# Two-layer transformer step on one Trainium2 core: the routed experts' rows gathered and combined in the experts' stage instead of a stage of their own

## What is computed

```python
xn = _layernorm(x, axis=-1)
s = _L1_attn_ref(xn)               # attention across the batch
g = _silu(_L1_ffn_ref(xn, ...))    # eight experts, two for each row
x = x + s * g
...
top_vals, top_idx = jax.lax.top_k(probs, K)            # K = 2 of E = 8
top_vals = top_vals / jnp.sum(top_vals, axis=-1, keepdims=True)
act = jax.nn.silu(h1) * h3
expert_out = jnp.einsum('tef,ehf->teh', act, w2)
y = jnp.einsum('te,teh->th', w_full, expert_out)       # weighted sum of the two
```

## Time and profile before

| | before |
|---|---|
| median of three runs | 1500.3 us |
| the profiled execution's own time | 1499.98 us |
| its span, first to last instruction | 1498.2 us |
| PE busy | 1346.3 us, 90% |
| DVE, ACT, POOL busy | 702.3, 565.6, 612.0 us |
| mean granted TensorE clock | 0.950 of full speed |
| last matmul ends, last gather is issued | 1441.34 us, 1485.96 us |

### The profile page before, as it was taken

The page is one execution under the profiler, slowest core; times in us unless marked ns, Lnnn a source line. Parts: engine busy times, 40 slices in busy tenths (PEclk is TensorE's granted clock), DMA queues, the critical chain, the costliest instruction groups (busy, mean ns, idle before and its releaser), DMA issues. The chain is left out here.

```text
span 1498.2 us, 25022 instructions
## 1 busy us (share of the span) xinstructions
PE 1346.3 (90%) x7870; PEld 1147.5 (77%) x7871; DVE 702.3 (47%) x1622; ACT 565.6 (38%) x1775; POOL 612.0 (41%) x518
## 2 busy tenths in 40 slices
PE   6989899999999999999885679999999999999940
PEld 6934487878787878887654569999999999999930
DVE  6452376666676766667636432223223222232236
ACT  3421276655556656655543321111212211112124
POOL 0010155444444545455426345172662617441135
PEclk9999899999999999999987789999999999999975
DMA  8025710000000000000015465373773828555247
GB/s 290 1 84 163 280 71 15 15 14 14 14 14 14 14 23 19 14 14 16 8 60 207 163 228 184 106 241 115 231 245 95 271 69 290 178 161 182 72 130 253
DMA packets 67069, 171.47 MB, mean 114 GB/s; under 512 B 6448, under 2 KB 15040, under 8 KB 66704
## 3 DMA queue, kind: packets, MB, share of 16 engines
q0 software_dynamic: 25776, 98.73, 19.8%
q1 hardware_dynamic: 35632, 61.95, 12.8%
q10 hardware_dynamic: 5616, 10.23, 1.9%
HBM read 125.26 MB, written 45.61 MB: 114 GB/s over the span
## 5 line engine op out<-in xcount | busy, mean ns | idle before, releaser
L1721 PE MATMUL bank<-expert_weights,rows_t 128*128 x1872 | 358.9, 347 | 2.1 <-DVE rows_t L1653 1.6
L1721 PEld LDWEIGHTS bank<-expert_weights,rows_t 128*128 128x128 f32 x1872 | 340.2, 189 | 6.1 <-issue 2.9
L989 ACT ACTIVATE room<-bank,room 128x256 f32<-128x256 f32 (+1 forms) x512 | 208.8, 415 | 115.5 <-DVE room L902 115.4
L1017 POOL TENSOR_TENSOR room<-room 128x1024 f32<-128x1024 f32 (+1 forms) x128 | 187.9, 1468 | 119.1 <-DVE room L879 119.1
L753 PE MATMUL bank<-room 96*128 (+2 forms) x1024 | 189.1, 327 | 0.0
L1665 DVE TENSOR_TENSOR x_keep<-x_keep,bank 128x400 f32<-128x400 f32 x78 | 44.5, 571 | 303.9 <-ACT x_keep L1608 302.6
L1131 POOL TENSOR_TENSOR expert_weights<-x_keep,expert_weights 128x1600 fp32r<-128x1600 f32 (+2 forms) x49 | 160.2, 3270 | 54.2 <-DMA expert_weights<-w 53.9
L753 PEld LDWEIGHTS bank<-room 96*128 96x128 f32 x1024 | 159.0, 191 | 13.7
L1744 PE MATMUL bank<-expert_weights,act_t 128*128 x702 | 165.6, 389 | 1.0 <-ACT act_t L1613 1.0
L1028 POOL TENSOR_TENSOR room<-room 128x256 f32<-128x256 f32 x128 | 93.1, 728 | 172.3 <-DVE room L963 171.1
L1744 PEld LDWEIGHTS bank<-expert_weights,act_t 128*128 128x128 f32 x702 | 131.5, 188 | 25.6 <-issue 1.3
(11 more groups left out here) (235 smaller groups left out, 1770.9 us busy)
## 6 DMA issues: line engine op xcount, KB each, us to landing
x_keep<-w POOLq DMA_DIRECT2D x28, 800.0 KB, 5.1
expert_weights<-w POOLq DMA_DIRECT2D x28, 800.0 KB, 6.5
x_keep<-w POOLq DMA_DIRECT2D x14, 768.0 KB, 5.7
expert_weights<-w POOLq DMA_DIRECT2D x14, 768.0 KB, 7.4
rows_by_expert<-room SPq DMA_DIRECT2D x1, 9984.0 KB, 29.1
x_keep<-rows_by_expert SPq DMA_DIRECT2D x39, 256.0 KB, 3.9
results_by_row<-x_keep ACTq DMA_DIRECT2D x39, 256.0 KB, 4.5
room<-wo SPq DMA_DIRECT2D x16, 512.0 KB, 5.7
```

What stands on the lines that cost most here:

```text
L989: last = sc.activation(Pr[:, m % 4, hh, 0:w], scores_bank(m)[:, w * hh:w * hh + w], ACT.Exp, bias=nb[:, par, hh:hh + 1], accum_out=sm[:, p ...
L1017: g.tensor_tensor(pr, pr, rs[:, one[1] % 2].unsqueeze(2).broadcast_to([P, 4, w]), ALU.mult).then_inc(normed, 1)
L1721: last = mm(psum(2 * hf + w)[:, 0:HF], xgT[:, par, of_x, P * k:P * k + P], W[:, ds(off + (of_w * SLOT + (k * 2 + w) * FF + hf * HF), HF)], ...
```

## The change

Stage `combine` goes. Its work stands in the experts' block, behind or beside the last blocks:

- A row's two places are stored in order of size, the lower expert's first (`s.slots`, two operations where there was one); its two weights are put in the same order by eight small DVE operations at the end of `across_batch`.
- Five more small DVE operations there make `s.landed`: how many results of even and of odd blocks have landed in DRAM when all before the last expert's have, and when all blocks in use have.
- POOL, behind its last weight chunk: when the results of all experts but the last have landed, it gathers the lower expert's rows of the 16 tiles into `z`, two gathers and then a wait for them; then it loads the attention results; when all blocks in use have landed, it gathers the first six tiles' rows of the higher expert, waits for the last block's `y_done`, and gathers the other ten.
- x1 is loaded by SP instead of POOL: one tile when the last rows are turned, three when the last activations are, the other twelve into buffers that come free as the tiles are added, each issued between two stores of the output.
- ACT scales six tiles ahead of the last block's copy out of PSUM and the other ten among the silus. DVE's three operations for a tile are those of before. `z`, the attention results and seven of the gathers' buffers lie over the first weight place.
- SP fills `ys` with zeros behind `xs`, and POOL's scatter waits for both. ACT's waits on `y_in` start from 16 more.

```diff
+                  ("by_parity", NBLK + 1),
...
+    put("by_parity", np.tile(np.concatenate([np.arange(0, NBLK + 1, 2), np.arange(1, NBLK + 1, 2)]), (P, 1)))
...
+        s.landed = s.carve(2, 2, dt=I32)
...
-        s.kept = sb(ctx, "kept", [P, 2, NT, D])
+
+        s.first_place = sb(ctx, "late", [P, 2 * SLOT])
         experts(s)
-        s.room(sb(ctx, "room3", [P, 10000]))
-        combine(s)
...
             sp.dma_start(s.xs.rearrange("(n p) h -> p n h", p=P),
                          zeros.unsqueeze(1).broadcast_to([P, NBLK, D])).then_inc(s.blank, 16)
+            sp.dma_start(s.ys.rearrange("(n p) h -> p n h", p=P),
+                         zeros.unsqueeze(1).broadcast_to([P, NBLK, D])).then_inc(s.blank, 16)
...
-            pool.wait_ge(s.blank, 16)
-            pool.wait_ge(slots_ready, 1)
+            pool.wait_ge(s.blank, 32)
+            pool.wait_ge(slots_ready, 2)
...
-            step(v.tensor_reduce(slotf[:, :, 0], small1, AX.X, ALU.add))
-            step.then(v.tensor_reduce(slotf[:, :, 1], small2, AX.X, ALU.add))
-            v.tensor_copy(s.slots, slotf).then_inc(slots_ready, 1)
+            step(v.tensor_reduce(slotf[:, 0], small1, AX.X, ALU.add))
+            step.then(v.tensor_reduce(slotf[:, 1], small2, AX.X, ALU.add))
+            v.tensor_tensor(s.slots[:, :, 0], slotf[:, 0], slotf[:, 1], ALU.min).then_inc(slots_ready, 1)
+            v.tensor_tensor(s.slots[:, :, 1], slotf[:, 0], slotf[:, 1], ALU.max).then_inc(slots_ready, 1)
...
+            ranked = s.gatew.rearrange("p t k -> p k t")
+            step(v.tensor_tensor(swap[:, 0], slotf[:, 0], slotf[:, 1], ALU.is_gt))
+            step(v.tensor_tensor(swap[:, 1], slotf[:, 0], slotf[:, 1], ALU.is_gt))
+            step(v.tensor_tensor(keep[:, 0], slotf[:, 0], slotf[:, 1], ALU.is_lt))
+            step.then(v.tensor_tensor(keep[:, 1], slotf[:, 0], slotf[:, 1], ALU.is_lt))
+            step(v.tensor_tensor(crossed[:, 0], ranked[:, 1], swap[:, 0], ALU.mult))
+            step(v.tensor_tensor(crossed[:, 1], ranked[:, 0], swap[:, 1], ALU.mult))
+            step.then(v.tensor_tensor(keep, ranked, keep, ALU.mult))
+            step(v.tensor_tensor(ranked, keep, crossed, ALU.add))
+
+
+            step(v.tensor_copy(until[:, 0:1], starts[:, E - 1:E]))
+            step.then(v.tensor_tensor(until[:, 1:2], starts[:, E - 1:E], n_blocks[:, E - 1:E], ALU.add))
+            step.then(v.tensor_tensor(below, until.unsqueeze(2).broadcast_to([P, 2, NBLK + 1]),
+                                      const("by_parity").unsqueeze(1).broadcast_to([P, 2, NBLK + 1]), ALU.is_gt))
+            step.then(v.tensor_reduce(n_below, below.rearrange("p i (r n) -> p i r n", r=2), AX.X, ALU.add))
+            step(v.tensor_scalar(s.landed, n_below, 16.0, 16.0, ALU.mult, ALU.add))
...
+    place = s.first_place
+    S = place[:, 0:NT * D].rearrange("p (t n) -> p t n", n=D)
+    z = place[:, NT * D:2 * NT * D].rearrange("p (t n) -> p t n", n=D)
+    def in_tiles(r):
+        return [r[:, i * D:i * D + D] for i in range(r.shape[-1] // D)]
+    higher = (in_tiles(place[:, 2 * NT * D:]) + in_tiles(stage.rearrange("p i n -> p (i n)")) +
+              in_tiles(s.carve(2 * D)) + [xg[:, 0]])
+    assert len(higher) == NT
+    x1_at = [xg[:, 1]] + in_tiles(act_.rearrange("p i n -> p (i n)"))
+    X1 = len(x1_at)
+    x1_at += higher[:NT - X1]
+    lower_in, scaled, gated, done, stored = (sem(n) for n in ("lower_in", "lower_scaled", "c_gated", "c_done", "stored"))
+    summed = sem("higher_added")
+    higher_in = [sem(f"higher_in{t}") for t in range(NT)]
+    x1_in = [sem(f"x1_in{i}") for i in range(X1)]
+    SCALED_FIRST, BESIDE_LAST = 6, 6
...
-            end = pool.value_load(s.ends[0:1, E - 2:E - 1], min_val=1, max_val=NBLK + 1)
-            pool.wait_ge(y_done, end)
-            pool.nop(nofuse=True)
+            def blocks_landed(which):
+                for par in range(2):
+                    n = pool.value_load(s.landed[0:1, which, par:par + 1], min_val=16, max_val=16 * (NBLK // 2 + 2))
+                    pool.wait_ge(y_in[par], n)
+                    pool.nop(nofuse=True)
+            def bring_rows(to, t, k, landed):
+                nc.gpsimd.indirect_dma_start(
+                    out=to, out_offset=None, in_=s.ys,
+                    in_offset=bass.IndirectOffsetOnAxis(ap=s.slots[:, t, k:k + 1], axis=0)).then_inc(landed, 16)
+            blocks_landed(0)
+            for t in range(NT):
+                bring_rows(z[:, t], t, 0, lower_in)
+                if t % 2 == 1:
+                    pool.wait_ge(lower_in, 16 * (t + 1))
             for q in range(NT // 2):
-
-                pool.wait_ge(y_done, NBLK - NT // 2 + q)
-                for i, rows in enumerate((s.x1, s.messages)):
-                    pool.dma_start(s.kept[:, i, 2 * q:2 * q + 2],
-                                   rows[2 * P * q:2 * P * q + 2 * P, :].rearrange("(t p) n -> p t n", p=P)).then_inc(
-                                       s.kept_in, 16)
+                pool.dma_start(S[:, 2 * q:2 * q + 2],
+                               s.messages[2 * P * q:2 * P * q + 2 * P, :].rearrange("(t p) n -> p t n", p=P)).then_inc(
+                                   s.kept_in, 16)
+            pool.wait_ge(s.converted, 1 + (E - 1) * NCH)
+            blocks_landed(1)
+            for t in range(NT):
+                if t == BESIDE_LAST:
+                    pool.wait_ge(y_done, NBLK + 1)
+                bring_rows(higher[t], t, 1, higher_in[t])
...
+            sp.sem_inc(y_in0, 16)
+            sp.sem_inc(y_in1, 16)
...
-            sp.wait_ge(y_in0, 16 * (NBLK // 2 + 1))
-            sp.wait_ge(y_in1, 16 * (NBLK // 2))
+            def bring_x1(t):
+                sp.dma_start(x1_at[t], s.x1[P * t:P * t + P, :]).then_inc(x1_in[t % X1], 16)
+
+            sp.wait_ge(x_turned, NBLK)
+            bring_x1(0)
+            sp.wait_ge(a_turned, NBLK)
+            for t in range(1, X1):
+                bring_x1(t)
+            for t in range(NT):
+                if t + X1 < NT:
+                    sp.wait_ge(summed, t + 1)
+                    sp.wait_ge(x1_in[t % X1], 16 * (t // X1 + 1))
+                    bring_x1(t + X1)
+                sp.wait_ge(done, 2 * t + 2)
+                sp.dma_start(s.out[P * t:P * t + P, :], z[:, t]).then_inc(stored, 16)
+            sp.wait_ge(y_in0, 16 + 16 * (NBLK // 2 + 1))
+            sp.wait_ge(y_in1, 16 + 16 * (NBLK // 2))
+            sp.wait_ge(stored, 16 * NT)
...
-                    act.wait_ge(y_in[1 - par], b * 8 - 8 if par == 1 else b * 8 - 16)
+                    act.wait_ge(y_in[1 - par], b * 8 + 8 if par == 1 else b * 8)
...
+            def scale(t):
+                sc.activation(z[:, t], z[:, t], ACT.Copy, scale=s.gatew[:, t, 0:1]).then_inc(scaled, 1)
+            act.wait_ge(lower_in, 16 * NT)
+            for t in range(SCALED_FIRST):
+                scale(t)
             result(NBLK, 1, False)
+            for t in range(NT):
+                if t + SCALED_FIRST < NT:
+                    scale(t + SCALED_FIRST)
+                act.wait_ge(summed, t + 1)
+                sc.activation(z[:, t], z[:, t], ACT.Silu).then_inc(gated, 1)
...
+            dve.wait_ge(s.kept_in, 16 * (NT // 2))
+            def add_higher(t):
+                dve.wait_ge(scaled, t + 1)
+                dve.wait_ge(higher_in[t], 16)
+                v.scalar_tensor_tensor(out=z[:, t], in0=higher[t], scalar=s.gatew[:, t, 1:2], in1=z[:, t],
+                                       op0=ALU.mult, op1=ALU.add).then_inc(summed, 1)
+            add_higher(0)
+            for t in range(NT):
+                if t + 1 < NT:
+                    add_higher(t + 1)
+                dve.wait_ge(gated, t + 1)
+                v.tensor_tensor(z[:, t], z[:, t], S[:, t], ALU.mult).then_inc(done, 1)
+                dve.wait_ge(done, 2 * t + 1)
+                dve.wait_ge(x1_in[t % X1], 16 * (t // X1 + 1))
+                v.tensor_tensor(z[:, t], z[:, t], x1_at[t], ALU.add).then_inc(done, 1)
...
-def combine(s):
...
```

More of the change, by code:

```diff
@@ L129, in build @@
         s.maskb = sb(ctx, "maskb", [P, P], BF16)
-        tables = sb(ctx, "tables", [P, 6 * NT + 2 * NBLK + E])
+        tables = sb(ctx, "tables", [P, 6 * NT + 2 * NBLK + E + 4])
         s.X = sb(ctx, "x_keep", [P, NT, D])
@@ L1149, in across_batch @@
     starts, of_block, odd = s.carve(E), s.carve(NBLK), s.carve(NBLK)
+    slotf, swap, keep, crossed = (s.carve(2, NT) for _ in range(4))
+    until, below, n_below = s.carve(2), s.carve(2, NBLK + 1), s.carve(2, 2)
     n_blocks = s.carve(E)
@@ L1163, in across_batch @@
     before_e, row_starts = s.carve(E, E), s.carve(E)
-    slotf, vals = s.carve(NT, 2), s.carve(NT, 2)
+    vals = s.carve(NT, 2)
     s.at = shared_at
@@ L1784, in _ @@
             down(NBLK - 1, place(NBLK - 1))
-def combine(s):
-    nc, sem, X, S = s.nc, s.sem, s.kept[:, 0], s.kept[:, 1]
-    DEEP = 5
-    yy = s.carve(DEEP, 2, D)
-    z = s.carve(4, D)
-    got = [sem(f"rows_got{i}") for i in range(DEEP)]
```

(43 more changed lines are left out.)

## The result

The changed kernel took 1474.11 us (median of 4 runs, 1472.43 to 1477.32) against 1499.45 us of the kernel before beside it; the ratio is 0.9842, 95% interval 0.9826 to 0.9859. Two later measurements of the same kernel gave 0.9855 [0.9838, 0.9872] and 0.9856 [0.9836, 0.9876] (medians 1475.69 and 1476.91, before 1497.93 both times). By these ratios it is faster by 21.6 to 23.7 us.

What follows compares the result with a forecast made beforehand. POOL's gathers and nearly full DMA engines were taken to bound the tail behind PE's last matmul. Tail -20.4, tables +2.0, late x1 +0.5 make -17.9 us: 1482.1 from the profiled 1499.98, put at 1482.4 for the median; range 1477.5 to 1489.

Steps and rivals of the forecast that it cites:

- The tail: Behind PE's last matmul: DVE's additions become the bound instead of POOL's gathers and the DMA engines, a gain of 20.4 us.
- cycle of three DVE operations: In the new tail: 14 tiles at 2.05 us each, 28.7 us together.
- The first addition: Start of the new tail: DVE's first addition of x1 starts at 1444.56, after ACT's first silu at 1443.05.
- term of 0.5: In the tail: x1 loads on SP come late once, by none to 3.2 us, taken as 0.5 us.
- Rival A: In the new tail: the DMA engines are the bound, giving 1480 us, or 1485 with x1 late; chance 0.12.
- rule of turns between queues: In the tail: engines alternate between queues with work, so x1 lands within its 9.0 us lead and costs no 0.5.
- The tables: Behind the last message, ahead of the experts: 13 new DVE operations are on the path in full, +2.0 us.
- the base: Whole kernel before: profiled execution 1499.98 us, 0.3 below the median of 1500.3, from which the gain was subtracted.
- lower end: Range's lower limit, whole kernel: 1477.5 us, with tables at nothing, cycle 2.00 and x1 never late.
- B: Tail: no higher gather runs beside the last block, 2.9 to 6.1 us more, 1485 to 1489; chance 0.08.
- C: Beside the last expert: gather pairs take far longer than 5.1 us, kernel slower from 11.9 a pair; chance 0.03.
- D: Start of attention: the second fill with zeros delays it by its full 29.1 us, giving 1511; chance 0.01.

Runs made afterwards that it cites:

- after_again: The changed kernel, unchanged, as a second profile and measurement: 1475.69 us, ratio 0.9855.
- tables_early: The changed kernel with all of DVE's table work moved from behind the last message to the fourth round of the layer-2 attention: 1476.76 us, ratio 0.9864.
- after_third: The changed kernel, unchanged, measured a third time: 1476.91 us, ratio 0.9856.
- none_beside: The changed kernel with BESIDE_LAST 0 instead of 6, so all 16 higher gathers stand behind the last block: 1481.0 us, ratio 0.9882.
- tables_x8: The changed kernel with the five operations for the table of landed results done eight times instead of once: 1483.38 us, ratio 0.9911.
- front edits: The kernel before with all edits of the stages ahead of the experts, experts and combine as before, measured three times: ratios 1.0001, 1.0024, 1.0005.
- front_again: The kernel before with all edits of the stages ahead of the experts, measured a second time: 1499.46 us, ratio 1.0024.
- lower_unpaired: The changed kernel with the lower expert's 16 gathers issued without the waits after every second one: 1489.25 us, ratio 0.9954.
- four `scatter` runs: POOL waiting after every 4, 8 or 16 scatters in the changed kernel: 1469.37, 1466.22, 1470.42 us; after every fourth in the kernel before: 1491.88 us.

## Why the prediction was wrong where it was

**The tail** was right in mechanism: POOL and the DMA engines bound it, now DVE does. It was off by 1.5 us: I forecast 36.4 + 0.5 and it is 35.4. Three terms were mis-sized. The cycle of three DVE operations is 1.99 us, not 2.05 (29.2 us from the first to the last addition of x1, not 30.1). The first addition starts 3.05 behind the last matmul, not 3.22. And x1 was not late in this profile, where I had put 0.5. That was close: loads landed in 2.6 to 8.6 us, against a lead of 9.0, and the chain that ended last holds one of them with 7.13 us. In `after_again` the slowest took 9.2 us and DVE waited 0.50, just the term, and in `tables_early` 0.9; in after_third and `none_beside` it waited for none. So the term of 0.5 belongs in the sum as a chance and not as a fixed price. Rival A is refuted as the bound, as DVE's cycle is 1.99 us in all of them. Its two numbers are also not of one kind: 1480 leaves out the 2.0 of the tables, 1485 has them in. The Trainium skill's rule of turns between queues ("DMA: Bandwidth & Descriptors", section "Queues, rings and completion order") had x1 landing inside the lead; most profiles agree with that, `after_again` and `tables_early` do not, and none singles the rule out.

**The tables.** The term was +2.0 and the new operations take 1.8 in the profile (864.83 to 866.67); that they are on the path is shown by `tables_x8`. The three measurements of the front edits (1.0001, 1.0024, 1.0005) average 1.5 us above before, with an interval of over 1 us either way. The term stands.

**The step that failed** is the one that the sum starts from, and with it a term that I had put at nothing without a reason: the spread of the stages ahead of the tail. I took the stretch ahead of the experts to have a fixed length. I read the profile of before, 1499.98 us, as the kernel's time, and its three runs' median of 1500.3 as the base. In 85 further runs, in four groups, before had medians of 1496.4 to 1497.9, so the base was 2.4 to 3.9 us too high. Of the 8.3 us between 1482.4 and 1474.1 the base makes at least 2.4, the tail 1.5 and the tables 0.5; of the 3.9 left, 1.6 to 2.8 went in the later medians of the same kernel. The range was too narrow at its lower end for the same reason. The terms that I named for that end (tables at nothing, cycle 2.00, x1 never late) come to 1479.2; the 1.7 us from there to 1477.5 have no term behind them, and none was for the base. From a base of 1497.9 the same sum gives 1480.0 and a range from 1475.1: the later medians (1475.69, 1476.91) lie in it and the first (1474.11) still does not, so part of the miss is the luck of four runs. The profiles show the spread in three places. The largest is ahead of the rounds: in profiles whose code is the same up to there, the matmuls at the end of layer 1 that wait for POOL (L766 in after) start anywhere from 738.0 (none_beside) to 742.6 us (tables_early), with a granted clock of 0.97 and 0.94 in the first 165 us. The second is where the rounds come to a stand under POOL's scatters, some 4 us between the fourth and the fifth. The third is PE's waits for weights (0.5 us in the profile of after, 2.9 in that of after_third, 4.3 in that of none_beside). The waits on remote and issue stood in the trace of before, and my prediction didn't ask what they were.

**The sum, redone**: tail -21.5, front +1.5, together -20.0. Measured differences by ratio: -23.7, -21.7, -21.6 us, each with an interval of 2.5 to 3 us either way. The last two contain -20.0; the first does not, by 1 us. Taken together they give -22.4, 1.5 either way, and -20.0 lies outside by 0.9; the front's own price is known to over 1 us only. Against the front edits measured beside it the changed kernel gains 21.9 and 22.3 us, which is the tail's 21.5 within the noise. What is left open, some 2 us, so lies with the price of the front edits, for which `front_again` gave 3.6 us and the other two 0.2 and 0.7. No run places it.

**Rivals.** B (`none_beside`) lost 5.3 us where 3 to 6 were worked out, of which 3.2 to 3.7 in the tail (2.9 worked out). C was the right place to fear, with the wrong mechanism: the pairs didn't take longer, but gathers without the pairs' waits would have cost 12 to 15 us through PE. D (the fill) didn't occur.

## What to carry to other kernels

When one engine issues many indirect DMAs back to back, look at the *other* engines for waits on issue or remote, and give the issuing queue a wait after every four or eight, if it has time to spare; here that brought 4 to 11 us in the medians for two lines. Idle time of that kind is room to put work in only in part: of 4.0 us, 2.2 to 2.9 came back. Measure a stage from its own start and not from the start of the span. And before a term of 2 us is argued from one profile, find out by how much the same stretch differs between two profiles of the same code.

## What was not expected of the hardware

With back-to-back indirect DMAs of 262 KB, issued by POOL every 1.27 us, PE, ACT and DVE stand, with little done in between, from 12 to 15 us behind the first until 4 to 5 us behind the last (before and `lower_unpaired`), while the DMA engines are 60% busy (0.60, 222 GB/s, 800 to 845 us in before). It happened with scatters to DRAM and with gathers from it, in straight code and inside a loop. Pauses of 2 to 5 us after four end it (0.72 busy at 240 GB/s, no stand). That the back-to-back indirect DMAs bring it about is shown by `lower_unpaired` and the four `scatter` runs. A pause both stops the issuing and lets what is under way land, and no run tells these apart.

How they do it is open. In the expectations I took it that the other engines' instructions come late. The rows of L1366 and L1701 above speak against that for DVE and ACT: these had their instruction and waited for a semaphore that was raised 12 to 18 us behind the recorded end of PE's matmuls, whether its signal or the matmuls themselves were late. For PE's single matmuls, which wait for nothing shown, late instructions stay possible. The Trainium skill says in "Runtime: NRT & Kernel Launch", section "Instruction fetch mechanics", that each engine's instruction memory is refilled in blocks by DMA. The traces have transfers of the kind "instruction", 58 in each of before and `lower_unpaired`, but none starts between 814 and 845 us in before, nor between 1345 and 1390 in `lower_unpaired`, where the engines stand; so they show no late refill.
